# A super-token attention and mixture-of-experts block: side visits, normalising and low halves in another order

## The reference

```python
x = x + conv_ref(_ln_c(x), ...)      # per image:
    aff = softmax(einsum('bnpc,bnck->bnpk', pix, unfold3(cell_means)) * scale)
    sft = fold3(einsum('bnpc,bnpk->bnck', pix, aff)) / (aff_sum + 1e-12)
    q, k, v = split(qkv_w @ sft);  out = proj_w @ softmax_attention(q, k, v) + proj_b
    pix_out = einsum('bnck,bnpk->bncp', unfold3(out), aff)
t = t + ffn_ref(_ln_t(t), ...)       # per pixel:
    masked = top2_of_4(softmax(t_n @ gate_w + gate_b)), renormalised
    h = gelu(t_n @ w1[e] + b1[e]);   y = h @ w2[e] + b2[e]     # 96 -> 384 -> 96
    out = sum over e of masked[e] * y[e]
```

## Time and profile before

| | |
|---|---|
| runs | 508.23, 507.08, 505.68 us; median 507.08 |
| profiled execution, its own time | 510.71 us |
| its span, first to last instruction | 508.9 us |
| mean granted TensorE clock | 0.933 of full speed |
| TensorE busy | 478.4 us, 94% |
| VectorE busy | 401.7 us, 79% |
| ScalarE busy | 332.9 us, 65% |
| GpSimd busy | 146.6 us, 29% |
| chain that ended last | TensorE 61%, VectorE 15%, ScalarE 10%, issue 7%, DMA 4% |

### The profile page before, as it was taken

One profiled execution on the slowest core, in us unless ns is written; L12 is line 12 of the kernel. 1 busy time (PEld: TensorE's weight loads), 2 busy tenths in 40 slices (PEclk: granted clock), 3 DMA queues, 4 the chain that ended last, 5 costly groups with the idle time before them and its releaser, 6 DMA issues.

```text
span 508.9 us, 13866 instructions
## 1 busy us (share of the span) xinstructions
PE 478.4 (94%) x5670; PEld 343.4 (67%) x5670; DVE 401.7 (79%) x1084; ACT 332.9 (65%) x317; POOL 146.6 (29%) x289
## 2 busy tenths in 40 slices
PE   9798979799999999999999999999999999899996
PEld 5697765586655777676666777677656676576665
DVE  7462792759997777999997777878899888969886
ACT  1023124737795676866795676867797978789983
POOL 4224011031088071031088071041127650123100
PEclk9757658989998999999998999999999999989999
DMA  8845214124212023424212022023251320221400
GB/s 232 292 142 154 52 32 95 33 48 68 48 33 57 17 48 48 98 48 67 48 33 56 18 48 49 3 48 67 48 78 26 48 50 4 48 48 35 69 17 21
DMA packets 68556, 31.45 MB, mean 62 GB/s; under 512 B 66462, under 2 KB 66598, under 8 KB 68101
## 3 DMA queue, kind: packets, MB, share of 16 engines
q1 hardware_dynamic: 67378, 28.27, 26.4%
q10 hardware_dynamic: 1114, 2.29, 1.3%
HBM read 12.33 MB, written 4.82 MB: 34 GB/s over the span
## 4 chain that ended last, share of the span: by engine, by line
PE 61%; DVE 15%; ACT 10%; issue 7%; DMA 4%; POOL 1%; SPq 0%; ACTq 0%; DVEq 0%; POOLq 0%
PE ps L1360 18%; PE ps L1388 13%; PE ps L1393 6%; ACT h L734 5%; PE ps L1235 5%; PE ps L1380 5%; PE ps L1222 4%; PE ps L1364 4%; ACT hh L742 4%; DMA xt<-xtok 3%; DVE xt L1073 3%; DVE hl L1057 3%; PE ps L1202 2%; DVE st L955 2%; DMA xhl<-x 2%
## 5 line engine op out<-in xcount | busy, mean ns | idle before, releaser
L734 ACT ACTIVATE h<-ps 128x1536 f32<-128x1536 f32 (+1 forms) x100 | 142.4, 1424 | 74.5 <-PE ps L1364 74.2
L1057 DVE TENSOR_TENSOR hl<-h,hh 128x1536 f16<-128x1536 f32 (+1 forms) x91 | 160.2, 1762 | 19.6 <-issue 19.5
L1073 DVE SCALAR_TENSOR_TENSOR xt<-ps,gl,xt 128x96 f32<-128x96 f32 (+1 forms) x400 | 99.8, 308 | 44.4 <-PE ps L1393 31.8
L742 ACT CAST hh<-h 128x1536 f16<-128x1536 f32 (+1 forms) x91 | 133.2, 1464 | 2.3
L520 POOL TENSOR_TENSOR x<-xs,x 128x384 f16<-128x384 f32 (+1 forms) x28 | 36.0, 1287 | 273.5 <-ACT x L700 273.5
L1388 PE MATMUL ps<-w_hi,hh 128*128 128x96 f16 x1092 | 107.2, 209 | 0.0
L1388 PE MATMUL ps<-w_lo,hh 128*128 128x96 f16 x1092 | 106.4, 208 | 0.0
L1388 PEld LDWEIGHTS ps<-w_hi,hh 128*128 128x128 f16 x1092 | 94.9, 100 | 11.1 <-issue 7.3
L1388 PEld LDWEIGHTS ps<-w_lo,hh 128*128 128x128 f16 x1092 | 96.1, 99 | 0.0
L1360 PE MATMUL ps<-xhl,w_a 128*128 128x512 f16 (+1 forms) x336 | 83.4, 357 | 5.2 <-DMA xhl<-x 5.2
L1360 PE MATMUL ps<-xhl,w_b 128*128 128x512 f16 (+1 forms) x336 | 83.6, 358 | 0.0
(11 more groups left out here) (165 smaller groups left out, 532.0 us busy)
## 6 DMA issues: line engine op xcount, KB each, us to landing
xch<-x SPq DMA_DIRECT2D x4, 1176.0 KB, 7.6
out<-xt SPq DMA_DIRECT2D x24, 192.0 KB, 2.8
xt<-xtok SPq DMA_DIRECT2D x4, 663.0 KB, 12.9
xt<-xtok SPq DMA_DIRECT2D x4, 612.0 KB, 11.2
h<-w ACTq DMA_DIRECT2D x2, 570.0 KB
h<-w ACTq DMA_DIRECT2D x1, 576.0 KB
xhl<-x SPq DMA_TRANSPOSE x28, 3.7
wqkv_sb<-wqkv ACTq DMA_DIRECT2D x1, 228.0 KB
```

Source lines behind the costliest of these rows:

```text
L734: act.activation(h32[:, i % 3, :, 0:width(i)], z, ACT.Gelu, scale=1.0 / WS).then_inc(S["h_ready"], 1)
L742: act.copy(hh[:, i % 3, :, 0:width(i)], h32[:, i % 3, :, 0:width(i)]).then_inc(S["hh_ready"], 1)
L1057: dve.tensor_tensor(hl[:, i % 2, :, 0:n], h32[:, i % 3, :, 0:n], hh[:, i % 3, :, 0:n], ALU.subtract).then_inc(S["hl_ready"], 1)
L1073: ins = dve.scalar_tensor_tensor(out=xt[0:n, b, t, 0:C], in0=ps[0:n, sum_bank(i), j * C:(j + 1) * C], scalar=gl[0:n, b % 2, t, e:e + 1], i ...
```

## The change

- The affinities of image 0 are turned by 25 TensorE transposes in four side visits (AFT 0 to 3, between SFT and PRT) and copied out of PSUM by ScalarE, instead of by the DMA of `turn_affinities(0)`; PIX of image 0 waits for these copies.
- Image 2's statistics move from slots 3, 4, 6, 7 and 8 of image 0 to the preparation; image 3's, in image 1, to slots 0, 3 and 4. The deviations on GpSimd follow them, to slot 0 (image 0) and 6 (image 1).
- `NORMAL`: units 2 to 6 are normalised at slots 1, 3, 4, 5, 8 instead of 2, 5, 8, 10, 12; unit 0 of the next image at 18 instead of 17 or 16.
- Side visits: PRT to PRO half a slot later; PIX at slots 11 to 17 in all images; the cell sums at slots 12, 14, 16, 18 instead of 15, 18, 18, 19, with CEN and the logits behind them.
- VectorE: in slots 13 to 17 (`AHEAD`) of images 0 to 2, pixels, their statistics and the addition come ahead of the next low half. In image 0 the quotient, the sums and the scaling come ahead of the additions of slots 1 and 2; in images 1 and 2 one block of sums moves to the slot 24 before, and the scaling from slot 1 to 0.
- ScalarE makes the high half ahead of side reads of half 0 and of the attention's tanh, and both `projected_again` copies come in slot 10.

```diff
--- before.py
+++ after.py
@@ -56,7 +56,9 @@
 
 FIRST_T = (0, 2 * TU, T)
 
-NORMAL = {2: 2, 5: 3, 8: 4, 10: 5, 12: 6}
+NORMAL = {1: 2, 3: 3, 4: 4, 5: 5, 8: 6}
+
+AHEAD = range(13, 18)
 
 SLOTS = (UNITS - 1) * E + 1
 
@@ -271,14 +273,15 @@
         Y, SIDE = 6, 7
 
         IDLE = 2
-        READER = {"SF": "act", "CEN": "act", "LOG": "dve", "SFT": "dve", "SUPT": "act", "QKV": "dve",
+        READER = {"SF": "act", "CEN": "act", "LOG": "dve", "SFT": "dve", "AFT": "act", "SUPT": "act", "QKV": "dve",
                   "SCO": "dve", "PRT": "act", "HEA": "dve", "HET": "act", "PRO": "dve", "PIX": "dve"}
 
 
         ROTATE = (SIDE, Y, 5, 4, 3)
         first = ([(0, "SF", k) for k in range(4)] + [(0, "CEN", 0)] + [(0, "LOG", k) for k in range(4)]
-                 + [(0, "SFT", 0), (0, "SUPT", 0), (0, "QKV", 0), (0, "SCO", 0), (0, "PRT", 0), (0, "HEA", 0),
-                    (0, "HET", 0), (0, "PRO", 0), (0, "PRO", 1)] + [(0, "PIX", u) for u in range(UNITS)])
+                 + [(0, "SFT", 0), (0, "AFT", 0), (0, "SUPT", 0), (0, "AFT", 1), (0, "QKV", 0), (0, "AFT", 2),
+                    (0, "SCO", 0), (0, "AFT", 3), (0, "PRT", 0), (0, "HEA", 0), (0, "HET", 0), (0, "PRO", 0),
+                    (0, "PRO", 1)] + [(0, "PIX", u) for u in range(UNITS)])
 
         then = {(0, "QKV", 0): [((1, "SF", 0), 0, 0, 2)], (0, "SCO", 0): [((1, "SF", 0), 0, 1, 2)],
                 (0, "PRO", 1): [((1, "SF", 1), 1, 0, 2)], (0, "PIX", 3): [((1, "SF", 1), 1, 1, 2)],
@@ -293,24 +296,22 @@
 
         EARLY = {(3, 1): (1, "SFT", 0, 0, 4), (4, 0): (1, "SFT", 0, 1, 4), (4, 1): (1, "SFT", 0, 2, 4),
                  (5, 0): (1, "SFT", 0, 3, 4), (5, 1): (1, "SUPT", 0), (6, 0): (1, "QKV", 0), (6, 1): (1, "SCO", 0),
-                 (8, 0): (1, "PRT", 0), (8, 1): (1, "HEA", 0), (9, 0): (1, "HET", 0),
-                 (9, 1): (1, "PRO", 0), (10, 0): (1, "PRO", 1), (11, 1): (1, "PIX", 0),
-                 (12, 1): (1, "PIX", 1), (13, 1): (1, "PIX", 2)}
-        TABLE = {**EARLY, (14, 1): (1, "PIX", 3), (15, 0): (2, "SF", 0), (15, 1): (1, "PIX", 4),
-                 (16, 1): (1, "PIX", 5), (17, 1): (1, "PIX", 6),
-                 (18, 0): (2, "SF", 1), (18, 1): (2, "SF", 2), (19, 0): (2, "SF", 3), (19, 1): (2, "CEN", 0),
-                 (20, 0): (2, "LOG", 0), (21, 0): (2, "LOG", 1), (21, 1): (2, "LOG", 2), (22, 0): (2, "LOG", 3)}
-
-        SHORT = {**EARLY, (14, 1): (1, "PIX", 3), (15, 1): (1, "PIX", 4),
-                 (16, 0): (1, "PIX", 5), (16, 1): (1, "PIX", 6)}
+                 (8, 1): (1, "PRT", 0), (9, 0): (1, "HEA", 0), (9, 1): (1, "HET", 0), (10, 0): (1, "PRO", 0),
+                 (10, 1): (1, "PRO", 1)}
+        EARLY.update({(11 + u, 1): (1, "PIX", u) for u in range(UNITS)})
+        TABLE = {**EARLY, (12, 0): (2, "SF", 0), (14, 0): (2, "SF", 1), (16, 0): (2, "SF", 2), (18, 0): (2, "SF", 3),
+                 (18, 1): (2, "CEN", 0), (19, 0): (2, "LOG", 0), (20, 0): (2, "LOG", 1), (21, 0): (2, "LOG", 2),
+                 (22, 0): (2, "LOG", 3)}
+
+        SHORT = EARLY
 
         def pixels_over(b):
 
-            return 17 if b + 2 < B else 16
+            return 17
 
         def unit_slots(b):
 
-            return pixels_over(b), 20
+            return 18, 20
 
         def side_at(b, slot, half):
 
@@ -463,8 +464,7 @@
             def turn_affinities(b):
                 sp.wait_ge(S["aff_hi"], 2 * b + 2)
                 sp.wait_ge(S["aff_lo"], b + 1)
-                if b > 0:
-                    sp.wait_ge(S["side_done"], number[(b - 1, "PIX", UNITS - 1)] + 1)
+                sp.wait_ge(S["side_done"], number[(b - 1, "PIX", UNITS - 1)] + 1)
                 sp.dma_start(affT[:], aff16[:], transpose=True).then_inc(S["aff_turned"], 16)
 
             def store(b, u):
@@ -473,7 +473,6 @@
                 sp.dma_start(out[first:first + n, :].rearrange("(t p) c -> p t c", p=min(n, PT)),
                              rows_of(b, u)[:, :, 0:C]).then_inc(S["out_stored"], 16)
 
-            turn_affinities(0)
             sp.wait_ge(S["pool_set"], 8)
             turn_tokens(0, 0)
             turn_tokens(0, 1)
@@ -484,7 +483,7 @@
                 for slot in range(SLOTS):
                     if slot - 2 in NORMAL:
                         turn_tokens(b, NORMAL[slot - 2])
-                    if b + 1 < B and slot == 6:
+                    if b + 1 < B and slot == 7:
                         turn_affinities(b + 1)
                     if slot % E == 0 and slot > 0:
                         store(b, slot // E - 1)
@@ -579,7 +578,7 @@
                             tokens_low(b + 1, unit_slots(b).index(slot - 1))
                         if slot == pixels_over(b) + 1:
                             pixel_deviation(b + 1, 1)
-                    if b + 2 < B and slot == 9:
+                    if b + 2 < B and slot == (0 if b == 0 else 6):
                         deviation(b + 2)
 
         @block.scalar
@@ -646,11 +645,22 @@
             def affinities_high(b):
                 act.wait_ge(S["aff_ready"], 2 * b + 2)
                 if b > 0:
-                    act.wait_ge(S["aff_turned"], b * 16)
+                    if b == 1:
+                        act.wait_ge(S["side_done"], number[(0, "AFT", 3)] + 1)
+                    else:
+                        act.wait_ge(S["aff_turned"], (b - 1) * 16)
                 else:
                     act.wait_ge(S["pool_set"], 6)
                 for zone in (0, 2):
                     act.copy(aff16[:, :, zone * ZONE:zone * ZONE + K9], affn[:]).then_inc(S["aff_hi"], 1)
+
+            def affinities_turned(b, k):
+                bank = opened((b, "AFT", k))
+                first = row_tiles(k)[0] * PT
+                n = min(IMG - first, TR * PT)
+                act.copy(affT[0:3 * ZONE, :, :].rearrange("k t p -> k (t p)")[:, first:first + n],
+                         bank[0:3 * ZONE, 0:n // 2].bitcast(F16)
+                         ).then_inc(S["side_act"], 1)
 
             def super_turned(b):
                 bank = opened((b, "SUPT", 0))
@@ -712,6 +722,8 @@
                     cells_summed(b, k)
                 elif kind == "CEN":
                     cells_centred(b)
+                elif kind == "AFT":
+                    affinities_turned(b, k)
                 elif kind == "SUPT":
                     super_turned(b)
                 elif kind == "PRT":
@@ -749,10 +761,14 @@
             affinity_exponentials(0, 1)
             affinities_high(0)
             scale_weights()
+            affinities_turned(0, 0)
             super_turned(0)
+            affinities_turned(0, 1)
             split_first_weights()
+            affinities_turned(0, 2)
             first_attention()
             cells_summed(1, 0)
+            affinities_turned(0, 3)
             probabilities_turned(0)
             heads_turned(0)
             for k in range(2):
@@ -777,12 +793,12 @@
                 if i + 2 < ALL:
                     hidden_full(i + 2)
                 after = divmod(i + 1, SLOTS) + (0,)
+                if i + 2 < ALL:
+                    hidden_high(i + 2)
                 if i + 1 < ALL and read_at(*after):
                     side_read(read_at(*after))
                 if b + 1 < B and slot == 6:
                     attention_tanh(b + 1)
-                if i + 2 < ALL:
-                    hidden_high(i + 2)
                 if slot - 1 in NORMAL:
                     tokens_high(b, NORMAL[slot - 1])
                 if b + 1 < B:
@@ -790,8 +806,9 @@
                         affinity_tanh()
                     if slot == 4:
                         affinities_high(b + 1)
-                    if slot in (9, 10):
-                        projected_again(b + 1, slot - 9)
+                    if slot == 10:
+                        projected_again(b + 1, 0)
+                        projected_again(b + 1, 1)
                     if slot - 1 in unit_slots(b):
                         tokens_high(b + 1, unit_slots(b).index(slot - 1))
                     if slot == 23:
@@ -1110,8 +1127,11 @@
             split_weights((1, 2))
             super_normalised(0)
             dve.wait_ge(S["pool_set"], 4)
+            statistics(2, 0, 6)
             queries(0)
+            statistics(2, 6, 12)
             shift_scores(0)
+            statistics(2, 12, T)
             finish_heads(0)
             split_weights((0,))
             projected(0, 0)
@@ -1136,38 +1156,38 @@
                 first, second = read_at(b, slot, 0), read_at(b, slot, 1)
                 if first and READER[first[1]] == "dve":
                     side_read(first)
-                late = slot == 7 and b + 1 < B
-                if late:
+                late = b + 1 < B and (slot == 7 or slot in AHEAD)
+                if slot == 7 and b + 1 < B:
                     attention_weights(b + 1)
-                elif i + 1 < ALL:
+                elif i + 1 < ALL and not late:
                     low_part(i + 1)
                 if second and READER[second[1]] == "dve":
```

(53 more changed lines are left out.)

## The result

Median of four runs 499.5 us (498.7 to 500.06), before 507.06 (505.68 to 508.23): ratio 0.984, interval 0.980 to 0.988, about 1.5% faster. The prediction was 500.7. Where a kernel shows two levels of time (c1 once, d1 in two of four executions, 1.5% above its fastest or more), its ratio is taken from the faster ones. The profiled execution of the changed kernel took 498.7 us (span 496.6), near its median; the one of before took 510.71, 3.6 over its median. So the two profiles differ by 12 us where the medians differ by 7.6.

The account below looks back on a forecast made before the run. The prediction took the time as TensorE's own work plus the places where it waits. Its terms summed to -6.4 us, from the 507.08 us median to 500.7 us (1.3% faster), range 493 to 506.5.

Parts of the forecast that it names:

- Preparation: Stage before image 0: transposes and copies add links to the attention chain, +0.8 us; bounds -1.5 to +2.
- Removing it gains nothing: Preparation: dropping image 0's affinity DMA saves no time, as its first reader is released later by VectorE's projection low part.
- Image 0, slots 1 to 4: Quotient, sums and scaling ahead of additions remove TensorE's wait for scaled affinities: -5.0 us, bounds 3 to 6 gained.
- TensorE then goes without a stop: Image 0: after slot 2's addition TensorE runs on without waiting, giving slot 3's result at 14.1 instead of 18.9 us.
- Slots 6 to 11: Images 0 to 2: statistics and a unit's normalising leave, gaining 1.5 us each in images 0 and 1, 0.3 in image 2.
- Cell sums: Images 0 and 1: pixels read ahead of the low half free the bank for later quarters, -3.6 us; bounds 0 to 5.
- Image 1: Slots 0 to 5: waits for slot 1's addition and the super tokens, plus two clock lowerings, +5.0 us; bounds +2 to +6.5.
- Image 2: Start, with half a lowering, +1.4 us; slots 11 to 24, wait for image 3's unit 0 tokens, +1.7 us.
- Image 3: Slot 6: earlier normalising of unit 2 removes TensorE's wait for its token DMA, -3.4 us; bounds 2.5 to 3.7 gained.
- The first (clock stays up): New waits in image 1, 2 and at the end bring no clock lowering: about 496 us; chance 0.25.
- the second's: Gains return as waits elsewhere: images 1 and 2 pay fully, slots 6 to 11 give only 1; 507.4 us; chance 0.12.
- the third's chain: Slots 13 to 17: additions ahead of low halves form one chain, 15 slots 1.1 us longer, near 517 us; chance 0.05.

Follow-up runs that it names:

- c1: Changed kernel with low half ahead of pixels and addition again in slots 13 to 17; median 504.79 us, ratio to before 0.989.
- d1: Changed kernel with dummy products on TensorE behind image 0's pixel visits and ahead of the first layer; median 503.63 us, ratio to before 0.981 from the faster two.
- a1: Changed kernel with image 0's affinities turned by the DMA again, without transposes and their copies; median 502.23 us.
- c2: Changed kernel with units 2 to 6 normalised in slots 2, 5, 8, 10 and 12 again; median 499.94 us.
- a2: Changed kernel with image 0's affinities turned by the DMA again and dummy products on TensorE where the transposes stood; median 500.16 us.
- g1: Changed kernel with units 2 to 6 of images 0 to 2 normalised in slots 2, 3, 5, 10, 12, image 3 as changed; median 496.4 us.
- b1: Changed kernel with image 3's statistics moved from image 1 to slots 10, 19, 20 and 23 of image 0; 495.21 us.
- b2: Changed kernel with unit 0 of image 3 normalised behind slot 17 instead of 18 of image 2; median 499.52 us.
- e1: Changed kernel with image 3's statistics in image 0, unit slots set by image, and unit 0 of image 3 behind slot 15; 494.3 us.

## Why the prediction was right, point by point

The total was right, the sum less so: against the profiles the terms give -6.4 and the traces -11.6. Of the gap, 3.6 us are the slow execution that the profile of before happened to be. So it is in part luck that 6.4 came within 1.2 us of the 7.6 between the medians: the terms were off by 0.3 to 2.6 us each, and the preparation's sign was wrong for the profile at hand. Two sums of the prediction do not come out either. The last of its shares gives 0.16 for "within", where its parts give 0.14. And two lowerings count as 2.4 us, where the row that it takes the price from gives 1.6 each.

- **Preparation, +0.8, measured -1.8** (-0.8 by the mean of the eight profiles). Two steps failed. "Removing it gains nothing" holds at half clock only: with the clock up TensorE waits 1.82 us for that DMA. And the lower bound of -1.5, a lifted clock, was as likely as not (four of eight profiles); where the clock fell early, the added links cost 1.7 to 2.0 us, near the upper bound. The Trainium skill, "TensorE: Matmul & The Clock Gate", section "Part 4: PE-mode transpose", says that the full clock does not engage for transposes, as they don't count as busy time in the same way. By it the clock should have fallen as with the DMA alone; it did so at 45 us in none of the eight profiles. But four fell at 47.5 or 50, where the one with ordinary products held, so whether transposes count for less stays open. The statistics in this stage cost nothing that I can show: a1, which has them and the DMA, reaches slot 0's addition at 86.8, before at 87.1.
- **Image 0, slots 1 to 4, -5.0, measured -3.6.** The mechanism held; the step "TensorE then goes without a stop" failed. I walked VectorE and did not compare slot 2's addition with TensorE's arrival: it came 1.5 us late, behind unit 2 (1.03) and a scaling of 1.98 in place of 1.24. Without unit 2 in slot 1 the wait is gone (29.30 us).
- **Slots 6 to 11, -3.3, measured -5.1.** Undersized. The unit slots account for 0.5 an image (c2), not 0.95. Before the change image 2, which has no statistics there, took 1.2 us less than images 0 and 1; now all three take 20.6. So the statistics, with the deviation that follows them, were 1.2 us of each of those two, and the last 0.4 an image was not separated.
- **Cell sums, -3.6, measured -5.5** over slots 11 to 25 of both images, with the 1.8 us in it that the sums add in the two slots 24. The forecast priced one slot, the one of 6.84 us, and took the order as what helps; the order gave 1.1 an image. A lowering in each of before's is gone too, so how much the spreading gave by itself stays open.
- **Image 1, +5.0, measured +4.5.** Two errors cancelled. The super tokens' wait was 2.15, not 1.1: unit 4's normalising took 1.86 beside GpSimd, not 0.95. And one lowering came, not two. Its price was 1.2 us, half of the 2.4 that stood for two: in the run with dummies (a2), where none followed the same wait, slots 0 to 6 took 31.50 instead of 32.72.
- **Image 2, +1.4 and +1.7, measured +0.7 and +2.3.** The mechanism held, the wait at slot 23 is 2.21, not 1.3. The prediction's own figures (15 and 3.7, less 17) give 1.7; the low parts ended 15.7 us behind slot 17's addition, and the DMA took 3.9. The clock stayed up behind it here, but fell in three of the eight profiles with this wait (a2, d1, g1), for 1.5 to 1.6 us.
- **Image 3, -3.4, measured -3.1.** The wait went. But with the old unit slots and no lowering behind the wait image 3 is only 1.3 longer; the other 1.8 is the lowering that the profile of before had there.
- **Rivals.** The first (clock stays up) is partly true, the second's waits came without its losses, the third's chain costs image 2 a little over 1 us and the others nothing.

## What to carry to other kernels

When work moves ahead of a hand-over, walk the engine that waits as well as the one that is rearranged; the first place that is late is the new price, and a place that pays in one stage (image 3, where VectorE is free) can cost more in the others. Compare versions stage by stage and not by one profile's total, as the same code of the preparation ended within a span of 4.8 us here, with the clock at different levels. And a transfer that is hidden by a slow stage can stop being hidden when that stage speeds up.

## What was not expected of the hardware

- The length of a wait does not settle whether the clock falls. The same wait of 1.50 us in image 0, slot 2, was followed by 0.50 in a1, b1 and c1 (slot 2 then took 5.8 instead of 4.16, so 1.6 us) and not in the changed kernel, a2, b2 and d1. The wait of 2.19 us in image 1 was followed by it in six profiles and not in a2's, c1's and g1's; the 2.15 us in slot 4 in none of seven. Whether that is chance, or follows from something that differs between the kernels, no run shows: b1's four executions all have a mean clock of 0.954, of e1's six four have 0.955 and two 0.942 or 0.943. In the images a lowering lasted 3.5 us each time (6.9 in slot 3 of before, 7.0 around c1's wait of 4.60) and cost 1.2 to 1.6.
- GpSimd stretches VectorE: scaling 1.98 us instead of 1.24, a unit's normalising 1.86 instead of 1.03, each by about the length of the GpSimd subtraction beside it (0.91 and 0.92). Not every GpSimd instruction does: in the kernel before a normalising at 140.98 took 1.20 us beside a copy and three short ones of GpSimd, 1.18 us in all. The Trainium skill, "GPSIMD Engine Reference", section "1. Specifications", says that its SBUF interfaces are shared with VectorE, with contention for VectorE instructions that have two SBUF inputs or run in a 2-port mode. The scaling has two such inputs, and its row agrees; for the normalising, which has one, no run shows the mode.
- The kernel before scatters between 505.7 and 513.3 us beside these runs, and that is of this kind too: the mean granted clock is 0.94 in the executions near 507 us and 0.93 in those over 509. The profiled one has 0.933; against 0.942 that is, by an estimate, 9 us more at half clock, two or three lowerings of 3.5 us, which at 1.2 to 1.6 us each are about the 3.6 by which it is slower.
